# Attention maxima combined in spare PSUM columns; first stage with a product and sum on VectorE, one sum of bias rows, and the context loaded first

## What is computed

```python
x = x + L0_xcond(cond, ctx, layernorm(x), ...)   # 3 rounds of attention from the tokens to the context, and a small MLP
x = x + L0_ffn(layernorm(x), ...)                # 8 experts, top 2
x = x + L1_xcond(ctx, layernorm(x), cond, cond)  # 16 heads of 64; keys are the 512 tokens and the 77 of the context
x = x + L1_ffn(layernorm(x), ...)                # 8 experts, top 1
x = x + L2_xcond(layernorm(x), cond, ctx, ...)   # self attention, cross attention, gated MLP
x = x + L2_ffn(layernorm(x), ...)                # 16 experts, top 2, two shared
x = x + L3_xcond(layernorm(x), cond, ctx, ...)   # 6 layers of self, cross attention (16 heads of 8) and MLP
x = x + L3_ffn(layernorm(x), ...)                # the routed half of the tokens through an MLP
```

```python
y  = z * exp(logsig) + mu                         # once, z is the normalised x
for _ in range(3):
    u = attention(layernorm(y), ctx) + y + bu
    m = gelu(layernorm(u) * g + b @ w1 + b1) @ w2
    y = layernorm(u + m + b2 + cond) * lnp_g + lnp_b
```

## Time and profile before

| | us |
|---|---|
| median of 3 runs | 4680.76 (4677.25 to 4685.16) |
| the profiled execution | 4679.2, of which span 4677.4 |

### The profile page before, as it was taken

One profiled execution on the slowest core, in us unless ns is written; L12 is line 12 of the kernel. 1 busy time (PEld: TensorE's weight loads), 2 busy tenths in 40 slices (PEclk: granted clock), 3 DMA queues, 4 the chain that ended last, 5 costly groups with the idle time before them and its releaser, 6 DMA issues.

```text
span 4677.4 us, 59467 instructions
## 1 busy us (share of the span) xinstructions
PE 3907.0 (84%) x23545; PEld 1763.7 (38%) x23545; DVE 2546.6 (54%) x4935; ACT 2428.6 (52%) x3409; POOL 1402.0 (30%) x1385
## 2 busy tenths in 40 slices
PE   5569899889897998898677688888888888888886
PEld 4347533333475334333344132333333332332333
DVE  4522354544223443543454867767777777677754
ACT  3634354344333545455211367666666667766674
POOL 3710134333101540341213232333333334332311
PEclk9679999999898999999788799999999999999998
DMA  1010000000000001000100101110110101111100
GB/s 50 0 56 1 37 5 19 15 9 16 33 1 27 19 19 36 8 19 29 64 2 24 40 22 29 37 43 22 43 37 22 57 23 40 40 29 35 36 11 14
DMA packets 103398, 124.78 MB, mean 27 GB/s; under 512 B 24883, under 2 KB 88571, under 8 KB 101192
## 3 DMA queue, kind: packets, MB, share of 16 engines
q1 hardware_dynamic: 103120, 120.99, 8.5%
HBM read 58.00 MB, written 1.45 MB: 13 GB/s over the span
## 4 chain that ended last, share of the span: by engine, by line
PE 64%; DVE 21%; ACT 7%; POOL 4%; issue 2%; DMA 1%; SPq 0%; POOLq 0%; DVEq 0%; ACTq 0%
PE ps L1765 8%; PE ps L1580 6%; PE ps L1564 5%; PE ps L1484 5%; PE ps L1476 5%; DVE c1sm L2434 3%; ACT wB L1991 3%; PE ps L1692 3%; DVE c0sm L2434 3%; PE ps L1751 3%; PE ps L1719 2%; PE ps L1612 2%; PE ps L1505 2%; PE ps L1800 2%; PE ps L1808 2%
## 5 line engine op out<-in xcount | busy, mean ns | idle before, releaser
L1991 ACT ACTIVATE wB<-ps 128x1024 f32<-128x1024 f32 (+1 forms) x775 | 776.5, 1021 | 302.1 <-PE ps L1751 295.7
L2434 DVE TENSOR_REDUCE c1sm<-ps 128x2 f32<-128x1024 f32 x384 | 460.3, 1221 | 110.5 <-PE ps L1719 107.2
L2434 DVE TENSOR_REDUCE c0sm<-ps 128x2 f32<-128x1024 f32 x384 | 461.0, 1221 | 107.9 <-PE ps L1719 104.8
L2279 DVE TENSOR_REDUCE c1sm<-ps 128x2 f32<-128x1024 f32 x128 | 155.5, 1223 | 282.2 <-PE ps L1529 281.7
L2279 DVE TENSOR_REDUCE c0sm<-ps 128x2 f32<-128x1024 f32 x128 | 155.2, 1221 | 144.1 <-PE ps L1529 143.9
L2538 POOL TENSOR_SCALAR c0ve<-c0mv 128x4 f32<-128x4 f32 (+1 forms) x29 | 6.7, 229 | 747.0 <-DVE c0mv L2058 743.4
L1991 ACT ACTIVATE c0m<-ps 128x1024 f32<-128x1024 f32 (+1 forms) x185 | 188.9, 1021 | 70.1 <-PE ps L1751 68.4
L2613 POOL TENSOR_TENSOR c0m<-c0m 128x512 f32<-128x512 f32 (+1 forms) x78 | 96.4, 1235 | 409.1 <-DVE c0m L2423 296.1
L1765 PE MATMUL ps<-wB,c0ar 128*9 128x512 f32 x1248 | 207.8, 620 | 12.5 <-ACT wB L1991 10.0
L1765 PE MATMUL ps<-wB,c1ar 128*9 128x512 f32 x1244 | 205.1, 610 | 14.2 <-ACT wB L1991 7.9
L1751 PE MATMUL ps<-c0ar 64*128 64x512 bf16 (+1 forms) x864 | 170.7, 394 | 48.6 <-DVE c1sm L2434 18.6
(11 more groups left out here) (692 smaller groups left out, 8817.3 us busy)
## 6 DMA issues: line engine op xcount, KB each, us to landing
c0ar<-c0m SPq DMA_DIRECT2D x216, 128.0 KB, 2.5
c1ar<-c0m SPq DMA_DIRECT2D x216, 128.0 KB, 2.4
c0m<-rscr SPq DMA_DIRECT2D x96, 128.0 KB, 2.9
c1m<-rscr SPq DMA_DIRECT2D x96, 128.0 KB, 2.9
wA<-in_lay SPq DMA_DIRECT2D x6, 1346.0 KB, 5.8
wA<-in_w SPq DMA_DIRECT2D x1, 4248.0 KB, 13.1
wA<-in_w SPq DMA_DIRECT2D x1, 4104.0 KB, 12.3
wA<-in_w4b SPq DMA_DIRECT2D x1, 2948.0 KB, 9.4
```

The lines of the kernel that those rows point to most:

```text
L1991: e.activation(P.ap[0:n, :, :], u.ap[0:n, :].rearrange("p (a q) -> p a q", a=2), ACT.Exp, scale=S8).then_inc(*A(("P8", n0, s, k), free=[u]))
L2279: e.tensor_reduce(c.sm[:, 2 * (g % 2), 2 * j:2 * j + 2], u.ap.rearrange("p (h k) -> p h k", h=2)[:, :, 0:n], AX, ALU.max, negate=True).the ...
L2434: e.tensor_reduce(c.mneg[:, s // 4, j, :, s % 4], u.ap.rearrange("p (a k) -> p a k", a=2), AX, ALU.max, negate=True).then_inc(*V(free=[u]))
```

## The change

In stages 2 and 4b the maxima over the context keys go to eight spare PSUM columns of the pair that held the scores, the minimum of both sets (they are negated maxima) to there too, and the cast and the remainder read from there; the pair is given back only after that. With one set of 512 keys (4a) the cast and remainder are a step of their own, `ms`. In stage 0 `s0p` goes from POOL to DVE; `b2 + cond` is added up once for all batches (`pre4`) and `s0base` makes one sum where it made two; the context is loaded first; its normalising, the small constants and the four streams' products are put in order by the planner, and `ln_z` of `x` no longer stands behind the context products in its stream. In all stages the planner's parameters, some of its costs, and the names of ACT's functions in chains are changed.

```diff
 ORDER = {
-    "0": dict(lag=0.3, weight=0.1, even=0.02, held=0.2, table=0.0, apart=20, spread=0.1, seed=7528),
+    "0": dict(lag=0.25, weight=0.0585, even=0.0178, held=0, table=0.2265, apart=0, spread=0.9215, seed=5133),
...
-    "6": dict(lag=0.1446, weight=0, even=0.0005, held=0.1686, table=1.3572, apart=62.1767, spread=0, seed=6779),
+    "6": dict(lag=0.1458, weight=0, even=0.0005, held=0.2113, table=1.4514, apart=62.8755, spread=0, seed=8180),
...
+        def constants():
+            first["eqs"] = yield from do("pre2", chain=[("A", .35, "exp")], after=10.0)
+            yield from do("pre3", chain=[("V", 1.0)], after=10.5)
+            yield from do("pre4", chain=[("V", .75)], after=10.5)
...
+            plan.spawn(values(), c)
+            z, t = yield from ln_z(c, xb(b), 5.7, "A")
+            while "eqs" not in first:
+                yield
+            t = yield from do("s0d", c, z, chain=[("V", 1.4)], after=max(t, first["eqs"]))
...
-                t = yield from do("s0p", c, n, it, z, chain=[("G", 2.6)], after=t)
+                t = yield from do("s0p", c, z, chain=[("V", 1.4)], after=t)
...
-                            (u,), t = yield Want([("T", .27), ("V", .73)], [two], tk_, True)
+                            (u,), t = yield Want([("T", .27), ("V", 1.2 + .25 * big)], [two], tk_, True)
                             emit("mxc", c, n0, g, o, n, u, big)
                             two.give(u, t[1])
-                    (u,), t = yield Want([("V", .6 + .25 * (len(segs) > 1)), ("T", .3), ("A", .6)], [banks], t[1])
-                    emit("mt", c, n0, g, big and len(segs) > 1, u)
+                    if len(segs) == 1 and big:
+                        t = yield from do("ms", c, n0, g, chain=[("V", .6)], after=t[1])
+                    (u,), t = yield Want([("T", .3), ("A", .6)], [banks], t)
+                    emit("mt", c, n0, g, u)
...
-        emit("pre2")
-        plan.stage("0")
-        plan.merge([stage0(c, c.i) for c in four] + [adaptive()])
+        plan.stage("0", four)
+        plan.merge([context(), constants()] + [stage0(c, c.i) for c in four] + [adaptive()], [None, None] + four)
...
             def pre():   # SP
+                e.dma_start(CT, d["ctx"]).then_inc(*D("ld_ctx")("ctx"))
                 e.dma_start(X, d["x"]).then_inc(*D("ld_x")("x"))
                 e.dma_start(CST, d["cst"]).then_inc(*D("ld_c")("c"))
+                e.dma_start(wB[:, 0:d["w0"].shape[1]], d["w0"]).then_inc(*D("w_w0")("w0"))
                 e.dma_start(MU8, d["mk"]).then_inc(*D("ld_m")("m"))
+                e.dma_start(MROW, d["mrow"]).then_inc(*D("ld_r")("r"))
                 e.dma_start(CTXT, d["ctxT"]).then_inc(*D("ld_t")("t"))
...
             def mxc(c, n0, g, o, n, u, big):   # DVE
+                m, more = u.ap[:, 480:488], u.ap[:, 488:496]
                 w.wait_ge(*T.at(("mxc", n0, g)))
+                e.tensor_reduce((more if big else m).rearrange("p (j h) -> p h j", h=2), v, AX, ALU.max, negate=True).then_inc(*V())
+                if big:
+                    w.wait_ge(*V.now())
+                    e.tensor_tensor(m, c.sm[:, 2 * (g % 2), 0:8], more, ALU.min).then_inc(*V())
+                    mss[c.i, g % 2] = V.n
+                split(c, n0, g, m, [u])
...
+            def split(c, n0, g, m, free=()):
+                mv = m.rearrange("p (j h) -> p j h", h=2)
...
                 e.tensor_copy(MS[:, :, :, 0], mv).then_inc(*V())
                 w.wait_ge(*V.now())
+                e.tensor_tensor(MS[:, :, :, 1], mv, MS[:, :, :, 0], ALU.subtract).then_inc(*V(("ms", n0, g), free=free))
...
             def s0base(c, key, row):   # POOL
                 base = v4(c.ar[:, 1700:2212])
+                w.wait_ge(*V.at("bc"))
+                e.tensor_tensor(base, c.y, bc4(row), ALU.add).then_inc(*G(key))
```

More of the change, by code:

```diff
@@ L562, in do, with context @@
             return t[-1]
+        first = {}
+        def context():
+            _, t = yield Want([("V", 1.35), ("G", 1.3)], after=5.5)
+            emit("cx0")
+            t = yield from do("cx1", chain=[("V", 1.15)], after=t[1])
+            (u,), t = yield Want([("T", .75), ("A", .45)], [banks], t)
+            emit("cx2", u)
+            banks.give(u, t[1])
+            first["cx"] = t[1]
+        def constants():
+            first["eqs"] = yield from do("pre2", chain=[("A", .35, "exp")], after=10.0)
+            yield from do("pre3", chain=[("V", 1.0)], after=10.5)
+            yield from do("pre4", chain=[("V", .75)], after=10.5)
         def stage0(c, b):
@@ L580, in stage0 @@
                 k = uid()
-                zt, key, tz = yield from ln_T(c, c.y, c.zT, t, None, None, "A", ("s0p", n, it - 1))
-                yield from do("s0base", c, ("base", k), (w["bu"],), None, chain=[("G", 1.3)], after=t)
-                (u,), t = yield Want([("T", .95), ("V", .9), ("A", .65), ("V", .9)], [banks], tz)
+                zt, key, tz = yield from ln_T(c, c.y, c.zT, t, None, None, "A")
+                yield from do("s0base", c, ("base", k), w["bu"], chain=[("G", 1.3)], after=t)
+                while b not in first:
+                    yield
+                (u,), t = yield Want([("T", .95), ("V", .9), ("A", .65, "exp"), ("V", .9)], [banks], max(tz, first[b]))
                 emit("s0s", c, k, n, zt, key, u)
@@ L603, in stage0 @@
                 z, t = yield from ln_z(c, c.y, t[1], "A")
-                t = yield from do("s0p", c, n, it, z, chain=[("G", 2.6)], after=t)
+                t = yield from do("s0p", c, z, chain=[("V", 1.4)], after=t)
                 c.z.give(z, t)
-            yield from do("xadd", c, b, ("s0p", n, 2), chain=[("V", .8)], after=t)
+            yield from do("xadd", c, b, chain=[("V", .8)], after=t)
         def adaptive():
@@ L2040, in pre, with pre3 @@
             def pre():
-                for k, x in (("ld_x", "x"), ("ld_c", "c"), ("ld_m", "m"), ("ld_t", "t"), ("ld_r", "r")):
+                w.wait_ge(*D("ld_x").at("x"))
+            def pre3():
+                for k, x in (("ld_c", "c"), ("ld_m", "m"), ("ld_r", "r")):
                     w.wait_ge(*D(k).at(x))
@@ L2102, in s0d, with s0p @@
                 e.tensor_tensor(c.y, c.y, bc4(W0["qmu"]), ALU.add).then_inc(*V())
+            def s0p(c, z):
+                w.wait_ge(*A.at(("z", z.n)))
+                e.tensor_tensor(c.y, z.ap, bc4(W0["lpg"]), ALU.mult).then_inc(*V(free=[z]))
+                w.wait_ge(*V.now())
+                e.tensor_tensor(c.y, c.y, bc4(W0["lpb"]), ALU.add).then_inc(*V())
             def s0s(c, k, n, zt, key, u):
@@ L2542, in cx0 @@
             def cx0():
-                ln(c0, "ctx", CT, NCTX)
+                ln(cx, "ctx", CT, NCTX)
             def pre2():
@@ L2552, in lnb, with s0base @@
                 e.tensor_tensor(c.ve, c.ve, c.rs, ALU.mult).then_inc(*G(("rs", n)))
-            def s0p(c, n, it, z):
-                w.wait_ge(*A.at(("z", z.n)))
-                e.tensor_tensor(c.y, z.ap, bc4(W0["lpg"]), ALU.mult).then_inc(*G(free=[z]))
-                w.wait_ge(*G.now())
-                e.tensor_tensor(c.y, c.y, bc4(W0["lpb"]), ALU.add).then_inc(*G(("s0p", n, it)))
-            def s0base(c, key, rows, _):
+            def s0base(c, key, row):
                 base = v4(c.ar[:, 1700:2212])
-                e.tensor_tensor(base, c.y, bc4(rows[0]), ALU.add).then_inc(*G(key))
-                for r in rows[1:]:
-                    w.wait_ge(*G.now())
-                    e.tensor_tensor(base, base, bc4(r), ALU.add).then_inc(*G(key))
+                w.wait_ge(*V.at("bc"))
+                e.tensor_tensor(base, c.y, bc4(row), ALU.add).then_inc(*G(key))
             def en(u):
```

136 lines of the change are left out of this document (66 added, 70 removed).

## The result

The changed kernel takes 4574.67 us (4572.2 to 4581.9) against 4679.01 us (4673.37 to 4685.16) of the kernel before in the same rounds: the ratio is 0.9779, 95% interval 0.9762 to 0.9797.

A forecast was written before the change was run, and what follows sets the result against it. Bound by PE's work plus idle time in stages 2 and 6, a chain of waits in stage 0. 4679.2 - 26 (stage 2) - 20 (rounds) - 23 (start) = 4610, with 1.6 for the median 4612 us; range 4580 to 4656.

The forecast's parts named there:

- Stage 2, the operands: Stage 2, minimum and remainder reading one operand from PSUM escape POOL's hold: 26 us gained, ends 38 and 8.
- The other two ways: Cross-checks of the stage 2 gain against 4a: PE's wait per combination gives 25 us, PE's idle share 29 us.
- Stage 2, the rest: Other seeds and costs shuffle every queue, and `ms` does what `mt` did: taken as 0.
- rival A: Stage 2: PE finds the pair not free or the maxima late, some 4 of 26 us left: 4634; chance 0.12.
- The pair held longer: Stage 2: minimum, cast and remainder pass before the pair is free: 0 taken, at worst 19 us lost, gain up to 5.
- writing PSUM: DVE writing or reading eight columns in PSUM: no difference from SBUF taken, 6 us either way.
- Stage 0, rounds: Stage 0's rounds with POOL relieved and two operations a round moved to DVE: 20 us gained, ends 4 and 30.
- Stage 0, start: Stage 0, context loaded first, first score matmul at about 35 instead of 61.9: 23 us gained, ends 5 and 32.
- rival B: Stage 0 gives little: `adaptive` ahead of context products leaves 5 us, DVE meeting POOL leaves 5 of 20: 4645; chance 0.12.
- Stage 4: Stages 4a and 4b: `ms` does what `mt` did, none of POOL's additions run in 4b: 0, within 5 us.
- Stage 6: Stage 6, 372 us of PE idle, partly decided by the order: 0 taken, 19 us either way.
- Rival C: Slower: stage 6's other order leaves PE idle longer in each of 24 layer passes, 3.5 us a pass: 4696; chance 0.06.

## Why the prediction was wrong, step by step

**Stage 2, the operands: right.** 28.5 us by the waits, 26 taken; 34.5 measured in the new order, of which 24.7 are PE's idle time, which is what was summed, and 9.8 PE's faster clock, which the sum did not have. Between the run with the cut step alone (670.4) and that with PSUM operands (646.3) lie 24 us, but there the order differs too, since DVE's part moved into the step of `mxc`. The other two ways, 25 and 29 us, agreed by luck: the stretch read as 4a, 1500 to 1800 us, is 4b from some 1710 on. It holds 25 combinations and not 16, and 7.8 of the 10.3 us of waiting are in 4b. 4a alone, in the kernel before:

```profile
1500.00:1700.00 200.00, 196.88 (x995) 71.37 (x993) 91.50 (x106) 116.25 (x165) 98.01 (x42) 1.00 0.06 17
...
PE ps L1551 <- DVE c0ar L2300: 1.7, 4, 0.4
```

With 2.5 us of waiting in 14 combinations the second way gives 32 x (1.43 - 0.18) = 40 us, and with 1.6% idle time the third gives 670 - 603.8/0.984 = 56. As estimates of what stage 2 would gain if it ran like 4a, they lie nearer to the measured 65 than to 26.

**Stage 2, the rest: the step that failed.** The prediction has it in the sentence on orders ("Other seeds and costs shuffle every queue") and in "`ms` does what `mt` did", at 0. Along one path the pieces are: the planner's step cut, 697.5 to 670.4, 27 us; PSUM operands, to 646.3, 24 us; new prices and parameters, to 632.5, 14 us. Along another they are 30.5 us for all that is order, 697.5 to 667.0, and then 34.5 for the operands. So what was put at 0 is 30 to 41 us. I read the diff of `mt` as a change of instructions, where it is also one of the order: while DVE's small operations and PE's transpose were one move, PE's queue got the transpose in one move with them, and PE then stood before it for 45.8 us. The row was there; I put all of that wait down to slow operations, and it was in part a place in a queue. What the new order does in the changed kernel itself is not shown, though: there the transpose has 6.5 us of matmul work ahead of it, no more than the 7.0 before, and the wait with SBUF operands was still 29.1 us in 19 places. That the one-operand form "turns the wait over" (rival A) did not happen.

**The pair held longer: right,** 0 taken, and freeing it early made stage 2 1.4 us longer, which is chance; **writing PSUM: right,** 171 and 806 ns against 161 in SBUF and some 800.

**Stage 0, rounds: right in size, for this order.** From the first score matmul to the end it was 253.2 - 61.9 = 191 us and is 228.1 - 57.4 = 171: 20 us, as forecast. 14.6 and 2.6 of them by the runs; the one sum is worth less than its share of POOL's relief, 15 of 47 us, suggested. That the edits alone bring this is not shown: with the old parameters the same code had rounds of 213 us. The meetings of DVE's moved operations with POOL's cost DVE little: 24 of them at 0.67 to 0.69 us but for three with a mean of 1.06, 1.1 us in sum. They cost POOL instead: 18 of its 121 operations on 128x4 at L2585, L2597 and L2599 took over 0.26 us, 7.5 us in sum above the undisturbed 0.195, and 16 of the 18 lay beside a moved operation (before: 3, 1.2 us). That is the 7 us estimated, on the other engine, and why POOL fell by 39 us and not by 47.

**Stage 0, start: the second step that failed,** 23 us forecast, 9.0 by the run that undoes it, 4.5 by the first score matmul (57.4 for 61.9). It went as rival B said, near the lower end of 5. The chain that ended last, in the profile after:

```profile
4.03 12.99 DMA wA<-in_ada
...
17.07 5.29 PE ps L1398 x24
24.06 5.00 PE ps L1398 x24
29.60 2.44 PE ps L1398 x12
32.98 5.14 PE ps L1398 x24
```

All seven groups stand at the head of PE's queue, with one stream's products between them. And I had looked at PE's queue alone: the scaling of `y` needs nothing of PE, but stands behind the last result of `adaptive` in DVE's queue, just as in the kernel before. The timeline after:

```profile
38.15 0.18 DVE L2190 TENSOR_TENSOR ADA<-ps,wA 128x24 f32<-128x24 f32 x1 [2.31 <-PE ps L1398]
38.24 0.68 DVE L2136 TENSOR_TENSOR c0m<-c0m,EQS 128x512 f32<-128x512 f32 x1
```

**Stage 4:** 0 within 5 us forecast, -16.1 measured, of which 14.7 are PE's busy time and 1.4 its idle time. The runs there span 824 to 860, and 19 us came with no change of order at all, so the bound was wrong, and whether the change is worth anything there stays open. **Stage 6:** 0 forecast and +4.1 measured, but the bound of 19 us had no row under it: the orders that were run lie between 2159 and 2232. Rival C, the slower side, was a real one. It decided from 69 us; the old parameters with the new prices cost 63.6, and with them the change as a whole is worth nothing (4683.6). I gave it 6 in 100, because the prices differ by so little. Whether it is the prices or the clocks handed on that spoil the old parameters stays open: in the runs with new prices in stage 6, stages ahead of it were different too, and an edit of stage 0 alone moved it by 16 us.

**The range** missed by 5 us on the fast side: it held each known part near its value and gave orders 10 us, where stage 2 alone got 30 to 41 us of order. That the whole came so near to the range is luck: stage 2 gave 39 us more than forecast and stage 0 18 less.

## What to carry to other kernels

When an edit touches a scheduler's steps or prices, take the order of the queues as an unknown of its own, and bound it by moving a parameter that means nothing in the kernel at hand; here that alone lengthens stage 6 of the kernel before by 52 to 55 us, half of the whole gain. Read a wait of a long queue twice: once for the slow instruction that it names, once for why the waiting instruction stood there. Before a stretch serves as the undisturbed case, see that it holds nothing else. Split the difference of a stage bound by PE into idle and busy time: here the busy time moved by 19 us with no instruction in another place. Small work on DVE beside long POOL instructions, two-operand work and casts from SBUF, reads from PSUM if columns are spare.

## What the runs showed of the hardware

In stage 2 PE's own time fell with its idle time. Of stage 2's 65 us 43 are less idle and 22 are the same 3280 instructions running faster; busy time and granted clock go together from run to run: 614 us at 0.94 before, 602 at 0.96 in the run with SBUF operands, 592 at 0.97 after. So the full speed of 2.4 GHz was granted for a larger share of the stage when PE waited less, and a wait taken away there paid half as much again as its length. The link is not strict: in the two runs of stage 4 in the same order PE idled 100 us in each, and was busy 724 us at 0.95 and 743 at 0.93. The busy time of stage 2 in the run with SBUF operands:

```profile
502.69:1169.64 666.95, 601.83 (x3280) 230.98 (x3280) 309.75 (x428) 309.54 (x497) 236.82 (x112) 0.96 0.06 20
```
